# Graph attention with one level of Strassen products: v's seventh product ahead of t's third, and another order of the prologue

## The chip, the cores and the metric

The kernel runs on one core of one Trainium2 chip. The metric is the device time of one execution in microseconds; several executions are made and their median is given.

## The reference

For each of 64 graphs of 128 nodes with 512 features (x is 64 x 128 x 512, adj 64 x 128 x 128):

```
h      = relu(layernorm(x))
output = h @ weight
alpha  = (h @ wq) @ (h @ wk)^T
alpha  = softmax(max(alpha, 0) * (adj != 0), over the first node axis)
result = x + alpha @ output
```

The three weights are 512 x 512 and everything is float32.

## The kernel before, in words

**Tiles and groups.** Four graphs make a group (GB = 4), so there are 16 groups, g = 0 to 15. The product of wq and wk^T is made once and called m; then t = h m and the scores are t h^T, while v = h weight. Each float32 operand of a matmul is split in two float16 parts, high and low (hn_hi and hn_lo for h, w_hi and w_lo, m_hi and m_lo, tT_hi and tT_lo, v_hi and v_lo, p_hi and p_lo for the probabilities), and each product is three matmuls: high by high, high by low, low by high. The high part is a rounding (a copy to float16), the low part is the difference.

**Strassen products.** For groups 2 to 14 t and v are made in quadrants by seven products each (P1 to P7) in place of eight. They need four sums of quadrants of h (S1 to S4, in s32), and of m and of weight (T1 to T4, in mt32 and wt32), each split in high and low as well. P7 is S3 by T3, P3 is S4 by a quadrant of the weights, P4 is a quadrant of h by T4. Between the products the banks are added: c22_t and c22_v are P1 + P6 + P7 + P5 of t and of v, made by DVE (lines 752 and 761) out of bank TB or VB, to which P4 is then added to form the last quadrant; so P4 of v waits for c22_v. Groups 0, 1 and 15 use whole products (whole_product_v, whole_product_t).

**The period.** One period of TensorE (g = 2 to 14) is: P1 and P5 of t, P1 and P5 of v, P2 and P6 of t, P2 and P6 of v, the four output products of the group before (outs), P7, P3 of t, P7 of v, P4 of t, P3 and P4 of v, and the scores. Around it in the same period, by orders written out by hand for each engine:

- ACT (from line 597) copies P1 and P5, makes the exponentials of the group before (line 579), rounds the quadrants of t and v (lines 540 to 570: t11, v11, t22, t12, v22, t21, v12, v21), makes h of group g+2 by the normalising activation (normalise_h, line 487), rounds it (hi_of_h, line 497) and rounds the sums of h (hi_of_sum, line 502).
- DVE (from line 799) masks the scores (alpha, line 776), takes the maxima (779), scales them (shift_max, 781), inverts the row sums (787, 792), takes the statistics of x for g+2 (721, 724), makes the sums of the products (747, 757, 752, 761), the low parts of t (735) and v (740), and adds the output to x (residual, 796).
- POOL normalises the probabilities (probs, p_hi, p_lo, lines 407 to 412), makes the scale and the shift of the layer norm (363 to 370), the low parts of h (375), the sums S1, S3, S2, S4 (383 to 394) and their low parts (401).
- SP issues all loads, the DMA transposes of the parts of h and of the mask, and the stores.

**The prologue.** Lines 636 to 694 of ACT, from 846 on in DVE, from 425 in POOL and from 1155 in TensorE: wk and wq are transposed, m is made in banks 0 to 3, power-of-two scales are found (w_scale is scale step 5, m_scale step 6), and w, m, T1 to T4 of both are split. DVE makes w_hi (892) and w_lo (894); ACT m_hi (650) and the float32 copy m32 (651), DVE m_lo (906); POOL the sums of w (440 to 446), DVE the sums of m (914 to 919); ACT rounds both, DVE takes the lows (wt_lo 927, mt_lo 936). TensorE makes v and t of group 0 (lines 1112 to 1114 and 1121 to 1123), scores of 0, t of 1, outs of 0, v of 1 (each waits for a residual of group 0, line 796, whose bank it takes), scores of 1, and then the first period. x_sb[:, 3] holds m32 until the sums of m are made; then x of group 3 is loaded into it.

Of the kernel before, what the change touches and what calls it, by code (L numbers as in the profile page):

```python
# [5 lines left out]
def graph_attention_kernel(nc, x, adj, weight, wq, wk, out):  # L6
# [18 lines left out]
    K = D // N  # L25
# [52 lines left out]
    with ctx:  # L78
# [88 lines left out]
        V_BANK = [[bank[VB][:], bank[VE][:], bank[FREE][:], s_flat if g == 0 else bank[TA][:]] for g in range(2)]  # L167
# [179 lines left out]
        def _(pool):  # L347
# [91 lines left out]
            pool.wait_ge(w_loaded, 16)  # L439
            nc.gpsimd.tensor_tensor(wt32[:, T1], w_sb[:, 0:HK, HD:], w_sb[:, 0:HK, :HD], ALU.subtract).then_inc(wt_summed, 1)  # L440
            nc.gpsimd.tensor_tensor(wt32[:, T3], w_sb[:, HK:, HD:], w_sb[:, 0:HK, HD:], ALU.subtract).then_inc(wt_summed, 1)
            pool.wait_ge(wt_summed, 1)
            nc.gpsimd.tensor_tensor(wt32[:, T2], w_sb[:, HK:, HD:], wt32[:, T1], ALU.subtract).then_inc(wt_summed, 1)
            layernorm_scales(1)
            pool.wait_ge(wt_summed, 3)
            nc.gpsimd.tensor_tensor(wt32[:, T4], w_sb[:, HK:, :HD], wt32[:, T2], ALU.subtract).then_inc(wt_summed, 1)
            for b in range(GB):
                lo_of_h(1, 1, b)
            layernorm_scales(2)
            sums_of_h(2, 0)  # L450
            normalise(0)
            lows_of_sums(2, 0)
# [20 lines left out]
        def _(act):  # L473
# [108 lines left out]
            def hi_of_whole_v(g, b):  # L582

                act.wait_ge(whole_v, whole(g, b + 1))
                if later(g):
                    act.wait_ge(out_filled, GB * g)
                nc.scalar.activation(v_hi[:, b], V_BANK[g > 0][b], ACT.Copy, scale=T_SCALE).then_inc(v_hi_made, 1)

# [8 lines left out]
            def period(i, j, nxt2=True, nxt2_sums=True):  # L597

                g = i * UNROLL + j
                s2 = (j + 2) % UNROLL  # L600

                def hi_of_h2(b):
                    hi_of_h(g + 2, j % 2, b, turn(i, j), sum_turn(i, j))

                copy_p1_t(g)
                exponentials(g - 1)
                copy_p5_t(g)
                copy_p1_v(g)
# [36 lines left out]


            act.wait_ge(scale_step, 6)
# [10 lines left out]
            for b in range(1, GB):  # L658
                hi_of_whole_v(0, b)
            act.wait_ge(wt_summed, 4)  # L660
            for f in range(4):
                nc.scalar.activation(wt_hi[:, f], wt32[:, f], ACT.Copy, scale=w_scale[:]).then_inc(wt_hi_made, 1)
            hi_of_whole_t(0, 0)
            hi_of_whole_t(0, 1)
            normalise_h(2, 2, 0)
            normalise_h(2, 2, 1)
            hi_of_whole_t(0, 2)
            normalise_h(2, 2, 2)
            normalise_h(2, 2, 3)
            hi_of_whole_t(0, 3)  # L670
            for b in range(GB):
                act.wait_ge(hT0_landed[b], 2 * 16)
                hi_of_h(2, 0, b)
            exponentials(0)
            act.wait_ge(mt_summed, 4)
            hi_of_whole_t(1, 0)
# [8 lines left out]
            hi_of_whole_t(1, 3)  # L685
            for b in range(GB):
# [4 lines left out]
            hi_of_whole_v(1, 0)  # L691
            hi_of_whole_v(1, 1)
            hi_of_sum(3, 1, 0, S1)
            hi_of_sum(3, 1, 1, S3)
            hi_of_whole_v(1, 2)
            hi_of_sum(3, 1, 2, S2)
            hi_of_sum(3, 1, 3, S4)
            hi_of_whole_v(1, 3)
# [15 lines left out]
        def _(vec):  # L714
# [120 lines left out]
            def lo_of_whole_v(g, b):  # L835
                vec.wait_ge(v_hi_made, GB * g + b + 1)
                nc.vector.scalar_tensor_tensor(v_lo[:, b], V_BANK[g > 0][b], T_SCALE, v_hi[:, b], ALU.mult,
                                               ALU.subtract).then_inc(v_split, 1)
# [20 lines left out]
            for b in range(GB):  # L859
# [28 lines left out]
            nc.vector.scalar_tensor_tensor(m_scale[:], ipow2[:, 1:2], m_factor, ipow2[:, 2:3], ALU.mult,  # L888
                                           ALU.mult).then_inc(scale_step, 1)
# [6 lines left out]
            stats_all(1, 1, 2)  # L896
            stats_all(1, 1, 3)
# [3 lines left out]
                                           pow2[:, 2:3], ALU.mult, ALU.mult).then_inc(scale_step, 1)  # L901
            for k in range(K):

                vec.wait_ge(m_hi_made, k + 1)
                vec.wait_ge(m_copied, k + 1)
# [4 lines left out]
            for b in range(GB):  # L910
                stats_all(2, 2, b)
            lo_of_whole_v(0, 0)

            nc.vector.tensor_tensor(mt32[:, T1], m32[:, 0:HK, HD:], m32[:, 0:HK, :HD], ALU.subtract).then_inc(mt_summed, 1)
            nc.vector.tensor_tensor(mt32[:, T3], m32[:, HK:, HD:], m32[:, 0:HK, HD:], ALU.subtract).then_inc(mt_summed, 1)
            vec.wait_ge(mt_summed, 1)
            nc.vector.tensor_tensor(mt32[:, T2], m32[:, HK:, HD:], mt32[:, T1], ALU.subtract).then_inc(mt_summed, 1)
            vec.wait_ge(mt_summed, 3)
            nc.vector.tensor_tensor(mt32[:, T4], m32[:, HK:, :HD], mt32[:, T2], ALU.subtract).then_inc(mt_summed, 1)
            for b in range(1, GB):  # L920
                lo_of_whole_v(0, b)
            for c in range(K):
                lo_of_whole_t(0, c)
            softmax_shift(0, 0, 1)
            for f in range(4):
# [39 lines left out]
        def _(pe):  # L965
# [73 lines left out]
            def period(i, j):  # L1039
# [66 lines left out]
            def whole_product_v(g, b):  # L1106

                s, dst = g % 2, V_BANK[g > 0][b]
# [36 lines left out]
            for b in range(GB):  # L1145
# [69 lines left out]
```

## Time and profile before

| what | us |
|---|---|
| median of 3 runs | 441.36 |
| lowest and highest run | 439.41, 442.39 |
| profiled execution | 444.44 |
| its span in the trace | 442.6 |
| TensorE busy | 412.1 |

The span is what the trace shows from the first to the last instruction; the time of the execution holds 1.8 us more around it. The granted TensorE clock was 0.987 of full speed over the span. Times in the rows are microseconds from the start of the span, "mean ns" and "ns" are said where they stand; PE is TensorE's matmul, DVE VectorE, ACT ScalarE, POOL GpSimd, SPq the queue of SyncE. An L with a number is a line of the kernel.

### The profile page before, as it was taken

The numbers are of one execution on the slowest core, as the hardware profiler recorded it, in microseconds if no ns is written. First come the engines' busy times: TensorE is split into PE (matmuls) and PEld (weight loads), VectorE is DVE, ScalarE is ACT, GpSimd is POOL, SyncE is SP. The second block draws the span as 40 slices with busy tenths as digits, with TensorE's granted clock in tenths as the row PEclk, the third lists the DMA queues.
The fourth block names the chain that finished last, engine by engine and source line by source line (L and its number), as shares of the span: only waits on it lengthen the run. The fifth ranks groups of instructions, "written<-read, shape, count | busy, mean of one in ns | idle before, by whom it ended". The sixth has DMA issues, their size and how long they took to land.

```text
span 442.6 us, 9188 instructions
## 1 busy us (share of the span) xinstructions
PE 412.1 (93%) x3499; PEld 313.9 (71%) x3499; DVE 300.6 (68%) x512; ACT 252.3 (57%) x513; POOL 296.7 (67%) x311
## 2 busy tenths in 40 slices
PE   6979894999999989999998999898998999899996
PEld 4424531497978777887978787787978787888452
DVE  4899499177677758677676768586676778637354
ACT  4548671648564665758565655748565655543331
POOL 0458497967779596987778795977778795320211
PEclk9989997899999999999999999999999999999999
DMA  8943755678869959798867879797787879263022
GB/s 300 327 86 59 205 109 121 185 145 196 195 171 176 240 143 182 226 160 249 156 193 163 200 173 208 168 182 236 138 194 167 192 180 219 44 96 108 0 97 96
DMA packets 157368, 73.97 MB, mean 167 GB/s; under 512 B 131216, under 2 KB 139408, under 8 KB 157328
## 3 DMA queue, kind: packets, MB, share of 16 engines
q1 hardware_dynamic: 156752, 72.37, 70.6%
q10 hardware_dynamic: 576, 1.05, 0.7%
q8 instruction: 27, 0.44, 0.4%
q14 instruction: 13, 0.11, 0.1%
HBM read 24.12 MB, written 16.78 MB: 92 GB/s over the span
## 4 chain that ended last, share of the span: by engine, by line
POOL 40%; PE 25%; issue 18%; DVE 9%; ACT 7%; DMA 1%; POOLq 0%; ACTq 0%; DVEq 0%
POOL hn_lo L375 12%; POOL hn_lo L401 8%; POOL s L390 4%; POOL inv_std L366 3%; POOL p_hi L410 3%; PE bank L1112 2%; PE bank L1114 2%; PE bank L1113 2%; POOL s L394 2%; POOL s L383 2%; ACT hn_hi L497 2%; ACT exps L579 2%; PE bank L1121 2%; PE bank L1122 2%; PE bank L1123 2%
## 5 line engine op out<-in xcount | busy, mean ns | idle before, releaser
L375 POOL TENSOR_TENSOR hn_lo<-h,hn_hi 128x512 f16<-128x512 f32 x64 | 79.3, 1249 | 39.4 <-ACT hn_hi L497 38.2
L487 ACT ACTIVATE h<-x_sb,shift,rstd 128x512 f32<-128x512 f32 x64 | 50.0, 806 | 59.7 <-POOL shift L370 59.7
L1002 PE MATMUL bank<-wt_hi,hT_hi 128*128 128x256 f16 x208 | 56.8, 273 | 10.2 <-DVE spare L761 10.2
L407 POOL TENSOR_TENSOR probs<-exps,row_inv 128x512 f32<-128x512 f32 x16 | 16.8, 1048 | 72.5 <-DVE row_inv L792 72.5
L740 DVE SCALAR_TENSOR_TENSOR v_lo<-bank,v_hi 128x512 f16<-128x512 f32 x39 | 26.7, 686 | 52.7 <-ACT v_hi L570 27.7
L401 POOL TENSOR_TENSOR hn_lo<-s,hn_hi 128x512 f16<-128x512 f32 x52 | 59.9, 1186 | 0.0
L1004 PE MATMUL bank<-wt_lo,hT_hi 128*128 128x256 f16 x208 | 56.7, 273 | 0.0
L1005 PE MATMUL bank<-wt_hi,hT_lo 128*128 128x256 f16 x208 | 56.7, 273 | 0.0
L987 PE MATMUL bank<-hT_hi,mt_hi 128*128 128x256 f16 x208 | 56.7, 273 | 0.0
L989 PE MATMUL bank<-hT_lo,mt_hi 128*128 128x256 f16 x208 | 56.7, 273 | 0.0
L990 PE MATMUL bank<-hT_hi,mt_lo 128*128 128x256 f16 x208 | 56.7, 273 | 0.0
L579 ACT ACTIVATE exps<-alpha,shift_max,s_unscale 128x128 f32<-128x128 f32 x64 | 30.9, 485 | 30.3 <-DVE shift_max L781 30.3
L1016 PE MATMUL s_bank<-tT_hi,hT_hi 128*128 128x128 f16 x256 | 43.7, 219 | 1.5 <-DVE tT_lo L842 1.5
L1017 PE MATMUL s_bank<-tT_lo,hT_hi 128*128 128x128 f16 x256 | 43.7, 219 | 0.0
L1018 PE MATMUL s_bank<-tT_hi,hT_lo 128*128 128x128 f16 x256 | 43.7, 219 | 0.0
L502 ACT ACTIVATE hn_hi<-s 128x512 f16<-128x512 f32 x52 | 32.0, 629 | 19.2 <-POOL s L390 10.8
L1004 PE MATMUL bank<-w_lo,hT_hi 128*128 128x256 f16 x156 | 42.5, 273 | 0.0
L1005 PE MATMUL bank<-w_hi,hT_lo 128*128 128x256 f16 x156 | 42.5, 273 | 0.0
L989 PE MATMUL bank<-hT_lo,m_hi 128*128 128x256 f16 x156 | 42.5, 273 | 0.0
L987 PE MATMUL bank<-hT_hi,m_hi 128*128 128x256 f16 x156 | 42.5, 273 | 0.0
L990 PE MATMUL bank<-hT_hi,m_lo 128*128 128x256 f16 x156 | 42.5, 273 | 0.0
L1002 PE MATMUL bank<-w_hi,hT_hi 128*128 128x256 f16 x156 | 42.5, 273 | 0.0
(148 smaller groups left out, 1165.4 us busy)
## 6 DMA issues: line engine op xcount, KB each, us to landing
x_sb<-in_x SPq DMA_DIRECT2D x16, 1024.0 KB, 5.6
out_h<-x_sb SPq DMA_DIRECT2D x64, 256.0 KB, 2.1
adj_sb<-in_adj SPq DMA_DIRECT2D x16, 256.0 KB, 5.3
w_sb<-in_L_gnn_weight SPq DMA_DIRECT2D x1, 1024.0 KB, 11.1
hn_lo<-in_L_gnn_wk ACTq DMA_DIRECT2D x2, 256.0 KB, 3.8
hn_lo<-in_L_gnn_wk SPq DMA_DIRECT2D x2, 256.0 KB, 3.6
hn_hi<-in_L_gnn_wq SPq DMA_DIRECT2D x2, 256.0 KB, 5.9
hn_hi<-in_L_gnn_wq ACTq DMA_DIRECT2D x2, 256.0 KB, 6.5
```

Of the source, the lines that this page charges most:

```text
L375: nc.gpsimd.tensor_tensor(hn_lo[:, s, b], h[:, b], hn_hi[:, s, b], ALU.subtract).then_inc(h_split, 1)
L401: nc.gpsimd.tensor_tensor(low, s32[:, f], high, ALU.subtract).then_inc(s_split, 1)
L487: nc.scalar.activation(h[:, b], x_sb[:, s, b], ACT.Relu, bias=shift[:, b:b + 1], scale=rstd[:, b:b + 1]).then_inc(h_made, 1)
L987: nc.tensor.matmul(o, bh[:, k, cols], ah[:, :, k], start=first and c == 0 and k == 0, stop=False, skip_group_check=True)
L989: nc.tensor.matmul(o, bh[:, k, cols], al[:, :, k], start=False, stop=False, skip_group_check=True)
L990: last = nc.tensor.matmul(o, bl[:, k, cols], ah[:, :, k], start=False, stop=k == HK - 1, skip_group_check=True)
L1002: nc.tensor.matmul(o, ah[:, r, k], bh[:, k], start=first and r == 0 and k == 0, stop=False, skip_group_check=True)
L1004: nc.tensor.matmul(o, ah[:, r, k], bl[:, k], start=False, stop=False, skip_group_check=True)
L1005: last = nc.tensor.matmul(o, al[:, r, k], bh[:, k], start=False, stop=k == HK - 1, skip_group_check=True)
L1016: nc.tensor.matmul(o, hT_hi[:, s, b, k], tT_hi[:, k, b], start=k == 0, stop=False)
L1017: nc.tensor.matmul(o, hT_hi[:, s, b, k], tT_lo[:, k, b], start=False, stop=False)
L1018: last = nc.tensor.matmul(o, hT_lo[:, s, b, k], tT_hi[:, k, b], start=False, stop=k == K - 1)
```

## The change

The arithmetic stays the same. Orders on all the engines change, and two kinds of operations move to another engine.

In the period, TensorE:

```diff
                 pe.wait_ge(t_summed, done(g, 1))
                 product_t(s, N_P7, bank[TB][:], False)
-                product_t(s, N_P3, bank[TE][:], False)
 
                 pe.wait_ge(v_summed, done(g, 1))
                 product_v(s, N_P7, bank[VB][:], False)
+                product_t(s, N_P3, bank[TE][:], False)
```

ACT and DVE in the period:

```diff
                     normalise_h(g + 2, s2, 1)
                     hi_of_h2(0)
                     normalise_h(g + 2, s2, 2)
+                hi_of_v11(g)
+                if nxt2:
                     hi_of_h2(1)
                     normalise_h(g + 2, s2, 3)
                     hi_of_h2(2)
-                    hi_of_h2(3)
-                hi_of_v11(g)
                 hi_of_t22(g)
                 hi_of_t12(g)
+                if nxt2:
+                    hi_of_h2(3)
                 if nxt2_sums:
                     hi_of_sum(g + 2, j % 2, 0, S1)
                     hi_of_sum(g + 2, j % 2, 1, S3)
+                hi_of_t21(g)
                 hi_of_v22(g)
-                hi_of_t21(g)
                 hi_of_v12(g)
                 if nxt2_sums:
                     hi_of_sum(g + 2, j % 2, 2, S2)
+                hi_of_v21(g)
+                if nxt2_sums:
                     hi_of_sum(g + 2, j % 2, 3, S4)
-                hi_of_v21(g)
```

```diff
                 sum_c22_t(g)
                 lo_of_v(g, 0, bank[VA][:], 0, 0)
+                sum_c22_v(g)
                 lo_of_t(g, 1, c22_t, 1, 1)
                 lo_of_t(g, 2, bank[TE][:], 0, 1)
-                sum_c22_v(g)
+                lo_of_t(g, 3, bank[TB][:], 1, 0)
                 lo_of_v(g, 1, c22_v, 1, 1)
-                lo_of_t(g, 3, bank[TB][:], 1, 0)
                 lo_of_v(g, 2, bank[VE][:], 0, 1)
                 lo_of_v(g, 3, bank[VB][:], 1, 0)
```

In the prologue ACT makes w_hi, and the copies of m come behind the roundings, the last one behind group 1's h:

```diff
+            act.wait_ge(scale_step, 5)
+            for k in range(K):
+                nc.scalar.activation(w_hi[:, k], w_sb[:, k], ACT.Copy, scale=w_scale[:]).then_inc(w_hi_made, 1)
 
             act.wait_ge(scale_step, 6)
             for k in range(K):
                 act.wait_ge(m_filled, k + 1)
                 nc.scalar.activation(m_hi[:, k], M_BANK[k], ACT.Copy, scale=m_scale[:]).then_inc(m_hi_made, 1)
-                nc.scalar.activation(m32[:, k], M_BANK[k], ACT.Copy, scale=m_scale[:]).then_inc(m_copied, 1)
-            hi_of_whole_v(0, 0)
+            for k in range(K - 1):
+                copy_m(k)
             for b in range(GB):
                 normalise_h(1, 1, b)
...
+            copy_m(K - 1)
```

POOL waits with the sums of w until the weights are split, and takes the sums of m over from DVE; normalising the probabilities of group 0 moves ahead of the second half of group 2's lows and sums:

```diff
-            pool.wait_ge(w_loaded, 16)
+            pool.wait_ge(w_split, K)
             nc.gpsimd.tensor_tensor(wt32[:, T1], w_sb[:, 0:HK, HD:], w_sb[:, 0:HK, :HD], ALU.subtract).then_inc(wt_summed, 1)
             nc.gpsimd.tensor_tensor(wt32[:, T3], w_sb[:, HK:, HD:], w_sb[:, 0:HK, HD:], ALU.subtract).then_inc(wt_summed, 1)
+            layernorm_scales(1)
             pool.wait_ge(wt_summed, 1)
             nc.gpsimd.tensor_tensor(wt32[:, T2], w_sb[:, HK:, HD:], wt32[:, T1], ALU.subtract).then_inc(wt_summed, 1)
-            layernorm_scales(1)
...
+            pool.wait_ge(m_copied, K)
+            nc.gpsimd.tensor_tensor(mt32[:, T1], m32[:, 0:HK, HD:], m32[:, 0:HK, :HD], ALU.subtract).then_inc(mt_summed, 1)
+            nc.gpsimd.tensor_tensor(mt32[:, T3], m32[:, HK:, HD:], m32[:, 0:HK, HD:], ALU.subtract).then_inc(mt_summed, 1)
+            pool.wait_ge(mt_summed, 1)
+            nc.gpsimd.tensor_tensor(mt32[:, T2], m32[:, HK:, HD:], mt32[:, T1], ALU.subtract).then_inc(mt_summed, 1)
             layernorm_scales(2)
-            sums_of_h(2, 0)
+            pool.wait_ge(mt_summed, 3)
+            nc.gpsimd.tensor_tensor(mt32[:, T4], m32[:, HK:, :HD], mt32[:, T2], ALU.subtract).then_inc(mt_summed, 1)
+            lo_of_h(2, 0, 0)
+            lo_of_h(2, 0, 1)
+            sum_s1(2)
+            sum_s3(2)
             normalise(0)
+            lo_of_h(2, 0, 2)
+            lo_of_h(2, 0, 3)
+            sum_s2(2)
+            sum_s4(2)
```

On DVE the scale of m comes behind w_lo; of group 1 the residuals of group 0 come ahead of mt_lo:

```diff
             vec.wait_ge(scale_step, 5)
             for k in range(K):
-                nc.vector.tensor_scalar(w_hi[:, k], w_sb[:, k], w_scale[:], None, ALU.mult).then_inc(w_hi_made, 1)
                 vec.wait_ge(w_hi_made, k + 1)
                 nc.vector.scalar_tensor_tensor(w_lo[:, k], w_sb[:, k], w_scale[:], w_hi[:, k], ALU.mult,
                                                ALU.subtract).then_inc(w_split, 1)
...
             lo_of_whole_t(1, 1)
+            lo_of_whole_t(1, 2)
+            lo_of_whole_t(1, 3)
+            for b in range(GB):
+                residual(0, 0, b)
             for f in range(4):
                 vec.wait_ge(mt_hi_made, f + 1)
                 nc.vector.tensor_tensor(mt_lo[:, f], mt32[:, f], mt_hi[:, f], ALU.subtract).then_inc(mt_split, 1)
-            lo_of_whole_t(1, 2)
-            lo_of_whole_t(1, 3)
             make_mask(2, 0, 2)
-            for b in range(GB):
-                residual(0, 0, b)
```

And TensorE takes the fourth whole product of v of group 0 (now in bank TA, no longer in s_bank) behind t's whole products:

```diff
-            for b in range(GB):
+            for b in range(GB - 1):
                 pe.wait_ge(hT0_landed[b], 2 * 16)
                 whole_product_v(0, b)
 
+            pe.wait_ge(hT0_landed[GB - 1], 2 * 16)
             pe.wait_ge(m_split, K)
             for c in range(K):
+                pe.wait_ge(m_copied, c + 1)
                 whole_product_t(0, c)
 
-            pe.wait_ge(v_split, 4)
+            pe.wait_ge(t_split, 1)
+            whole_product_v(0, GB - 1)
             scores(0, 0, quadrants=False)
+
+            pe.wait_ge(v_split, GB)
```

The roundings and lows of groups 0 to 3 on ACT and DVE are put in an order that answers to this.

## Rows read from the trace of the kernel before

**Rows 1.** The page, busy time of each engine, share of the span, instructions.
```profile
PE 412.1 (93%) x3499; PEld 313.9 (71%) x3499; DVE 300.6 (68%) x512; ACT 252.3 (57%) x513; POOL 296.7 (67%) x311
```

**Rows 2.** Waits of TensorE: line, releaser, us in total, times, longest.
```profile
PE bank L1002 <- DVE spare L761: 10.2, 11, 1.5
```

**Rows 3.** Timeline of TensorE: start, duration, line, output and inputs, [idle before, releaser].
```profile
90.62 0.27 PE L987 MATMUL bank<-hT_hi,m_hi 128*128 128x256 f16 x1
...
101.10 0.38 PE L1023 MATMUL bank<-v_hi,p_hi 128*128 128x512 f16 x1
...
111.55 0.22 PE L1016 MATMUL s_bank<-tT_hi,hT_hi 128*128 128x128 f16 x1
...
114.23 0.27 PE L987 MATMUL bank<-hT_hi,m_hi 128*128 128x256 f16 x1
...
160.01 0.28 PE L1002 MATMUL bank<-wt_hi,hT_hi 128*128 128x256 f16 x1 [1.49 <-DVE spare L761]
...
184.12 0.28 PE L1002 MATMUL bank<-wt_hi,hT_hi 128*128 128x256 f16 x1 [0.32 <-DVE spare L761]
...
407.16 0.22 PE L1016 MATMUL s_bank<-tT_hi,hT_hi 128*128 128x128 f16 x1
```

**Rows 4.** Timeline of POOL, the first probs and one turn of the ring.
```profile
95.13 1.04 POOL L407 TENSOR_TENSOR probs<-exps,row_inv 128x512 f32<-128x512 f32 x1 [3.57 <-DVE row_inv L792]
...
169.92 1.04 POOL L407 TENSOR_TENSOR probs<-exps,row_inv 128x512 f32<-128x512 f32 x1 [1.54 <-DVE row_inv L792]
...
184.96 1.71 POOL L390 TENSOR_TENSOR s<-s,h 128x512 f32<-128x512 f32 x1
186.75 1.27 POOL L394 TENSOR_TENSOR s<-h,s 128x512 f32<-128x512 f32 x1
187.98 4.52 POOL L401 TENSOR_TENSOR hn_lo<-s,hn_hi 128x512 f16<-128x512 f32 x4
194.04 1.04 POOL L407 TENSOR_TENSOR probs<-exps,row_inv 128x512 f32<-128x512 f32 x1 [1.54 <-DVE row_inv L792]
```

**Rows 5.** Timeline of ACT in the same turn.
```profile
180.27 0.58 ACT L558 ACTIVATE v_hi<-bank 128x512 f16<-128x512 f32 x1
...
188.05 0.63 ACT L502 ACTIVATE hn_hi<-s 128x512 f16<-128x512 f32 x1 [0.72 <-POOL s L394]
```

**Rows 6.** Timeline of DVE, the same turn and one slower shift_max.
```profile
189.81 0.68 DVE L776 SCALAR_TENSOR_TENSOR alpha<-s_bank,maskT 128x512 f32<-128x512 f32 x1
...
191.25 0.23 DVE L781 TENSOR_SCALAR shift_max<-row_max,s_unscale 128x4 f32<-128x4 f32 x1
...
215.52 1.12 DVE L781 TENSOR_SCALAR shift_max<-row_max,s_unscale 128x4 f32<-128x4 f32 x1
```

**Rows 7.** The prologue: timelines of DVE, ACT, SP, TensorE; landing of hT_lo; a window with PEclk.
```profile
30.46 0.75 DVE L894 SCALAR_TENSOR_TENSOR w_lo<-w_sb,w_scale,w_hi 128x512 f16<-128x512 f32 x1
...
56.60 6.58 DVE L927 SCALAR_TENSOR_TENSOR wt_lo<-wt,w_scale,wt_hi 128x512 f16<-128x512 f32 x4
...
20.85 1.14 ACT L497 ACTIVATE hn_hi<-h 128x512 f16<-128x512 f32 x2
...
29.45 1.27 SPq L278 DMA_TRANSPOSE hT_lo<-hn_lo  x1
...
DMA to landing us min/median/max: 2.5/2.5/4.5
...
25.91 0.38 PE L1112 MATMUL bank<-w_hi,hT_hi 128*128 128x512 f16 x1 [1.02 <-DVE w_lo L894]
...
28.90 0.61 PE L1112 MATMUL bank<-w_hi,hT_hi 128*128 128x512 f16 x1 [2.18 <-DVE w_lo L894]
...
40.11 0.38 PE L1121 MATMUL bank<-hT_hi,m_hi 128*128 128x512 f16 x1
...
75.51 0.59 PE L1112 MATMUL bank<-w_hi,hT_hi 128*128 128x512 f16 x1 [5.86 <-DVE x_sb L796]
...
75.00:80.00 5.00, 4.49 (x12) 1.65 (x13) 2.34 (x4) 4.66 (x8) 2.69 (x5) 0.53 0.87 266
```

More of the change, by code:

```diff
@@ L166, in graph_attention_kernel @@
         M_BANK = [bank[k][:] for k in range(K)]
-        V_BANK = [[bank[VB][:], bank[VE][:], bank[FREE][:], s_flat if g == 0 else bank[TA][:]] for g in range(2)]
+        V_BANK = [bank[VB][:], bank[VE][:], bank[FREE][:], bank[TA][:]]
         def out_bank(g):
@@ L586, in hi_of_whole_v @@
                     act.wait_ge(out_filled, GB * g)
-                nc.scalar.activation(v_hi[:, b], V_BANK[g > 0][b], ACT.Copy, scale=T_SCALE).then_inc(v_hi_made, 1)
+                nc.scalar.activation(v_hi[:, b], V_BANK[b], ACT.Copy, scale=T_SCALE).then_inc(v_hi_made, 1)
             def hi_of_whole_t(g, c):
@@ L644, in _, with copy_m @@
             hi_of_h(0, 0, GB - 1)
+            def copy_m(k):
+                act.wait_ge(m_split, k + 1)
+                nc.scalar.activation(m32[:, k], M_BANK[k], ACT.Copy, scale=m_scale[:]).then_inc(m_copied, 1)
+            act.wait_ge(scale_step, 5)
+            for k in range(K):
+                nc.scalar.activation(w_hi[:, k], w_sb[:, k], ACT.Copy, scale=w_scale[:]).then_inc(w_hi_made, 1)
             act.wait_ge(scale_step, 6)
@@ L657, in _ @@
             hi_of_h(1, 1, GB - 1)
-            for b in range(1, GB):
-                hi_of_whole_v(0, b)
+            copy_m(K - 1)
+            hi_of_whole_t(0, 0)
+            hi_of_whole_v(0, 0)
+            hi_of_whole_v(0, 1)
+            hi_of_whole_t(0, 1)
+            hi_of_whole_v(0, 2)
             act.wait_ge(wt_summed, 4)
-            for f in range(4):
+            for f in range(2):
                 nc.scalar.activation(wt_hi[:, f], wt32[:, f], ACT.Copy, scale=w_scale[:]).then_inc(wt_hi_made, 1)
-            hi_of_whole_t(0, 0)
-            hi_of_whole_t(0, 1)
+            hi_of_whole_t(0, 2)
+            for f in range(2, 4):
+                nc.scalar.activation(wt_hi[:, f], wt32[:, f], ACT.Copy, scale=w_scale[:]).then_inc(wt_hi_made, 1)
+            hi_of_whole_t(0, 3)
             normalise_h(2, 2, 0)
             normalise_h(2, 2, 1)
-            hi_of_whole_t(0, 2)
+            hi_of_whole_v(0, 3)
+            act.wait_ge(hT0_landed[0], 2 * 16)
+            hi_of_h(2, 0, 0)
+            act.wait_ge(hT0_landed[1], 2 * 16)
+            hi_of_h(2, 0, 1)
             normalise_h(2, 2, 2)
             normalise_h(2, 2, 3)
-            hi_of_whole_t(0, 3)
-            for b in range(GB):
-                act.wait_ge(hT0_landed[b], 2 * 16)
-                hi_of_h(2, 0, b)
             exponentials(0)
+            act.wait_ge(hT0_landed[2], 2 * 16)
+            hi_of_h(2, 0, 2)
+            act.wait_ge(hT0_landed[3], 2 * 16)
+            hi_of_h(2, 0, 3)
+            hi_of_whole_t(1, 0)
             act.wait_ge(mt_summed, 4)
-            hi_of_whole_t(1, 0)
             for f in range(4):
@@ L685, in _ @@
             hi_of_whole_t(1, 3)
+            hi_of_whole_v(1, 0)
             for b in range(GB):
@@ L690, in _ @@
             hi_of_h(3, 1, GB - 1)
-            hi_of_whole_v(1, 0)
             hi_of_whole_v(1, 1)
+            hi_of_whole_v(1, 2)
             hi_of_sum(3, 1, 0, S1)
             hi_of_sum(3, 1, 1, S3)
-            hi_of_whole_v(1, 2)
+            hi_of_whole_v(1, 3)
             hi_of_sum(3, 1, 2, S2)
             hi_of_sum(3, 1, 3, S4)
-            hi_of_whole_v(1, 3)
             period(0, FIRST)
@@ L836, in lo_of_whole_v @@
                 vec.wait_ge(v_hi_made, GB * g + b + 1)
-                nc.vector.scalar_tensor_tensor(v_lo[:, b], V_BANK[g > 0][b], T_SCALE, v_hi[:, b], ALU.mult,
+                nc.vector.scalar_tensor_tensor(v_lo[:, b], V_BANK[b], T_SCALE, v_hi[:, b], ALU.mult,
                                                ALU.subtract).then_inc(v_split, 1)
@@ L887, in _ @@
             nc.vector.tensor_scalar(w_scale[:], ipow2[:, 0:1], w_factor, None, ALU.mult).then_inc(scale_step, 1)
-            nc.vector.scalar_tensor_tensor(m_scale[:], ipow2[:, 1:2], m_factor, ipow2[:, 2:3], ALU.mult,
-                                           ALU.mult).then_inc(scale_step, 1)
             vec.wait_ge(scale_step, 5)
             for k in range(K):
-                nc.vector.tensor_scalar(w_hi[:, k], w_sb[:, k], w_scale[:], None, ALU.mult).then_inc(w_hi_made, 1)
                 vec.wait_ge(w_hi_made, k + 1)
@@ L895, in _ @@
                                                ALU.subtract).then_inc(w_split, 1)
-            stats_all(1, 1, 2)
-            stats_all(1, 1, 3)
+            nc.vector.scalar_tensor_tensor(m_scale[:], ipow2[:, 1:2], m_factor, ipow2[:, 2:3], ALU.mult,
+                                           ALU.mult).then_inc(scale_step, 1)
             nc.vector.tensor_scalar(out_unscale[:], pow2[:, 0:1], 1.0 / (P_SCALE * H_SCALE * T_SCALE * w_factor), None,
@@ L901, in _ @@
                                            pow2[:, 2:3], ALU.mult, ALU.mult).then_inc(scale_step, 1)
+            stats_all(1, 1, 2)
+            stats_all(1, 1, 3)
+            vec.wait_ge(scale_step, 6)
             for k in range(K):
                 vec.wait_ge(m_hi_made, k + 1)
-                vec.wait_ge(m_copied, k + 1)
                 nc.vector.scalar_tensor_tensor(m_lo[:, k], M_BANK[k], m_scale[:], m_hi[:, k], ALU.mult,
@@ L911, in _ @@
                 stats_all(2, 2, b)
+            lo_of_whole_t(0, 0)
             lo_of_whole_v(0, 0)
[L914 to L923, printed above, removed]
+            lo_of_whole_v(0, 1)
+            lo_of_whole_t(0, 1)
+            lo_of_whole_v(0, 2)
+            for f in range(2):
+                vec.wait_ge(wt_hi_made, f + 1)
+                nc.vector.scalar_tensor_tensor(wt_lo[:, f], wt32[:, f], w_scale[:], wt_hi[:, f], ALU.mult,
+                                               ALU.subtract).then_inc(wt_split, 1)
+            lo_of_whole_t(0, 2)
+            lo_of_whole_t(0, 3)
+            lo_of_whole_v(0, 3)
+            vec.wait_ge(scale_step, SCALE_STEPS)
             softmax_shift(0, 0, 1)
-            for f in range(4):
+            for f in range(2, 4):
                 vec.wait_ge(wt_hi_made, f + 1)
@@ L1106, in whole_product_v @@
             def whole_product_v(g, b):
-                s, dst = g % 2, V_BANK[g > 0][b]
+                s, dst = g % 2, V_BANK[b]
                 for k in range(K):
@@ L1143, in _ @@
             product_m(3)
-            for b in range(GB):
+            for b in range(GB - 1):
                 pe.wait_ge(hT0_landed[b], 2 * 16)
                 whole_product_v(0, b)
+            pe.wait_ge(hT0_landed[GB - 1], 2 * 16)
             pe.wait_ge(m_split, K)
             for c in range(K):
+                pe.wait_ge(m_copied, c + 1)
                 whole_product_t(0, c)
-            pe.wait_ge(v_split, 4)
+            pe.wait_ge(t_split, 1)
+            whole_product_v(0, GB - 1)
             scores(0, 0, quadrants=False)
+            pe.wait_ge(v_split, GB)
             pe.wait_ge(hT_landed[1], 2 * 16)
```

## The prediction

> **What bounds the kernel now.** I read the page first, for which engine is full; then the waits of TensorE, for what stops it; then the timeline of TensorE, for the length of a period; then the timelines of the other engines over one period, for what releases it; last the prologue.
>
> TensorE is busy for 412.1 of 442.6 us, so what it loses in waits is nearly all there is to win without fewer matmuls [rows 1]. Its longest sum of waits is 10.2 us in 11 pieces: the first matmul of v's last product (P4) waits for c22_v, DVE's sum of line 761 [rows 2]; three more, of 5.86, 2.18 and 1.02 us, lie in the prologue [rows 7]. The period of g=2 has no wait: it starts at 90.62, its outs at 101.10, its scores at 111.55, and the next period at 114.23 [rows 3]. So eight products take 10.48 us, 1.31 each (12 matmuls, 0.109 each; one of 512 columns then 0.218), and a period that never waits takes 23.61. The thirteen periods with sums run from 90.62 to the scores of the last at 407.16; 13 times 23.61, less 2.68 for those scores, is 304.25, and the trace has 316.54: 12.3 us are lost in eleven of them (a wait is some 0.16 longer than its row, as the row counts from a modelled end). Two rows show both sizes, 1.49 and 0.32 [rows 3].
>
> What releases the wait is a ring of the other engines. From probs to probs POOL takes 24.12 us (169.92 to 194.04) [rows 4], which is 0.5 more than TensorE needs. Its links: POOL normalises the probabilities and makes the scale of the layer norm; ACT makes h and, only behind all eight operations on h, v_hi of the first quadrant at 180.27 [rows 5]; DVE then takes v_lo, two lows of t and c22_v. Meanwhile POOL goes through lows and sums of h to the end of S2 at 186.67 and of S4 at 188.02 [rows 4]; ACT rounds S4 at 188.05 and only then v21 [rows 5]; DVE's v_lo and then alpha follow at 189.81, though the scores, started 1.31 after the product of 184.12 and 2.68 long, had been there since about 188.2; shift_max, the exponentials and row_inv lead to the next probs [rows 4, 6]. In other periods shift_max takes 1.12 to 1.26 instead of 0.23 [rows 6], and the wait one product later in the ring is the long one. It began at 215.52 while POOL was within its four lows of sums, each 1.13; I read it as waiting for the one in progress. The Trainium skill, "SBUF — State Buffer", section "Who interferes with whom", says the same: a tensor_scalar in a two-port mode and an instruction with two SBUF inputs contend with GpSimd for one locked pair. By that rule moving mt's four sums to POOL frees DVE but buys new collisions with DVE's wt_lo; the trace agrees that such operations stretch.
>
> **Part 1, the product order in the period (thirteen times).** Nothing is added or taken on any engine; P7 of v ends one product, 1.31 us, earlier, at 15.7 instead of 17.0 us after the period's start; t's P3 ends 1.31 later. More matters the ACT order: v_hi of the first quadrant comes behind four operations on h instead of eight, some 2.3 us earlier (a rounding is 0.57 [rows 7]), and DVE takes c22_v straight after that v_lo, ahead of two lows of t (0.7 each by the nearest row, alpha [rows 6]). So c22_v comes at least 3.7 us sooner in the ring where the longest wait was 1.65. The wait goes. P4 then waits for nothing but the products before it, with some 2 us in hand.
>
> What is late next is the ring. ACT now rounds S4 behind v21, which waits for S2 only: S2's end instead of S4's, 1.35 us sooner. Against this, v_hi stands before the second rounding of h, so POOL's second low starts some 0.5 later (it now starts just when that rounding ends), and everything on POOL after it too. Alpha comes 0.85 sooner, 19.04 us behind probs where it was 19.89. shift_max, three links on, then falls in POOL's second low of a sum rather than near the end of the third; waiting for its end costs up to 0.3. The ring becomes 24.12 - 0.85 + 0.3, about 23.6, against TensorE's 23.61. That is a draw, and the slack decides: probs may come between 4.4 (scores bind) and 6.9 us (the second half of the scores needs the last low of t) after the start of a period before TensorE waits at all, so single slow turns are absorbed. Bounds: no wait left gives 12.3 us; a ring of 24.1 gives back 0.5 times 12, leaving 6. A ring that always misses a slot is a rival below. I take 2 us of remaining waits: **10.3 us won**.
>
> **Part 2, the prologue.** DVE now makes w_lo only, ACT w_hi, and POOL waits until the weights are split. The last w_lo of DVE ended at 31.21; TensorE, whose products of M end at 24.9, idled 1.02 and 2.18 us for the first two and then ran at 0.61 a matmul where 0.38 is usual [rows 7]. Now ACT's four w_hi (0.6 each, by its roundings of 0.57) run from 22.0, when group 0's last h is rounded, to 24.5 [rows 7]; w_lo's end at about 24.5, 25.2, 25.9 and 26.6. TensorE can go on almost without idling; the 3.2 us of waits and the slow matmuls after them go. Then the transposes of h are late next: the last is issued at 29.45 and takes 2.5 to land, 31.95 [rows 7]. Three whole products of v (2.6 each) run from 24.9 to 32.7, and as the fourth moves behind t's products, the first t product starts there if m is split. m_scale, now behind w_lo, comes at 26.7; ACT's m_hi end at 29.1; DVE's statistics and four m_lo end at 32.3, or 33.4 if m_scale waits for POOL. So t's products start at 32.7 to 33.4 where they did at 40.11 [rows 7]: 7 us sooner. m_copied of the last column comes behind group 1's h on ACT, at about 37.8, and is needed at 40.5: covered.
>
> From there TensorE has t (10.4), v's fourth (2.6), scores (2.7), t of group 1 (10.4) and outs (2.6): 28.7 us, so outs end at 61.4 if probabilities are there at 58.8. POOL's list (mt's sums 5.0, layer norm 2.0 to 2.7, T4, two lows, S1, S3) ends at 53; normalise gives p_lo at 57.3. Covered, by 1.5 us only; it starts this list at 38.9, when group 1's lows end (four lows of 1.13 behind the eight ACT operations on h, 5.0 us, which end at 37.2).
>
> Then v of group 1 needs the residuals of group 0. They stood behind four mt_lo of 5.42 us in all, and v began at 75.51 after 5.86 us idle [rows 7]. Now they come ahead of mt_lo but behind the last low of t, which on ACT is behind the rounding of S4: POOL's two lows, S2 and S4 end at 62.1, ACT and DVE need 1.8, a residual 0.7: v starts at 64.6, idle 3.2 us. Bounds: 63.0 if nothing collides, 67 if POOL's dozen operations each lose 0.3. The clock fell after the idle of before: 0.53 was granted from 75 to 80, the lower of the two levels, 1.2 and 2.4 GHz [rows 7]. I keep 2.1 us for it. Products 10.4, scores 2.7: the first period starts at 79.8 instead of 90.62. v_lo of group 1 (needed first) is at 79.3, mt_lo at 72.6; POOL's lows of group 3's sums end at 86.3, and probs with them (95.13 before [rows 4]): 6.4 us after the period's start, just inside the 6.9. **10.7 us won**, 7 to 13.5.
>
> **Part 3, the tail.** From the last period's scores at 407.16 to the end nothing is changed and TensorE was dense: 35.4 us stay.
>
> **Sum.** The profiled execution took 444.44 us with a span of 442.6. 444.44 - 10.3 - 10.7 = 423.4. The median of the runs, 441.36, is 3.1 us under the profiled one, which I keep: 420.4. Predicted: 420.5 us, 4.7% faster.
>
> **Rivals.**
> A, the ring stays the bound. For it: probs comes in only 0.5 us inside the limit at the first period, and 23.6 against 23.61 is closer than I can add. If each turn is 24.1 to 24.3 (the half microsecond on POOL's second low and a missed slot every second turn), 6 to 8 us are given back to TensorE's wait for the last t low or for p_lo: 426 to 428. Against it: TensorE's slack. 0.22.
>
> B, the prologue gives little. If m's split, POOL's list or group 0's residuals come 4 us later than I have them, the first period starts near 84 or 85: 425. For it: DVE's wt_lo collide with POOL there (6.58 us for four before). 0.12.
>
> C, the idle goes altogether, residuals by 62, clock never low: 415 to 417. 0.08.
>
> D, slower. POOL and DVE block each other more in the new order: the ring loses a whole slot of 1.13 twice each turn (shift_max, and one of DVE's two operations with two SBUF inputs, the lows of c22_t and c22_v, against S1 to S2). Place: alpha to probs and S1 to S2 on POOL. From a ring of 25.4 on, twelve turns eat the 8.8 us by which probs starts earlier (12 times 24.7 was the old average, 0.7 above is 8.4). At 25.9 it is 12 times 1.2 less 8.8: 447. For it, the stretched shift_max; against, that these collisions are in the 24.7 already. 0.03.
>
> E, the wait moves without gain because P3 of t now feeds its rounding late and holds up h's fourth rounding on ACT behind it: within 1%, 440. Against: that rounding comes at 18.1 us of the period where POOL wants it at about 20. 0.03.
>
> **How the numbers follow.** My case has 0.52, with its own range of 417 to 425. A, B and C fill up to 430 and down to 415; range 414 to 431. One per cent, 4.4 us, is about what the measurement can tell. Faster 0.94, same 0.03, slower 0.03.
>
> **What would show it.** Right: no wait of TensorE at P4 of v for c22_v; period starts 23.6 apart; first period at about 80; t's whole products from about 33; one wait near 62 to 65 ended by a residual. shift_max still long in some turns with TensorE unmoved. Wrong: period starts over 24.0 apart, with TensorE released by p_lo or t_lo (A); the first period after 83 (B).

## The result and the profile after

| what | us |
|---|---|
| changed kernel, median of 4 runs | 421.12 (420.80 to 421.59) |
| kernel before, median of 4 runs | 440.91 (439.41 to 442.39) |
| ratio | 0.9552, 95% interval 0.9517 to 0.9587 |
| profiled execution, and its span | 420.80, 419.0 (before 444.44, 442.6) |

The change makes the kernel 4.5% faster; 420.5 was forecast. Ratios here and below are those of the fast runs (less than 1.5% above the kernel's fastest), so they differ a little from the quotients of the medians shown. The page's busy times, against [rows 1]:

```profile
PE 406.6 (97%) x3499; PEld 314.8 (75%) x3499; DVE 282.9 (68%) x504; ACT 253.3 (60%) x517; POOL 298.2 (71%) x315
```

TensorE has the same 3499 matmuls and is now busy for 97% of the span. DVE has eight operations fewer (four w_hi, four sums of m) and ACT and POOL four more each. These are TensorE's waits, against [rows 2]:

```profile
PE bank L1121 <- DMA hn_lo<-in_L_gnn_wk: 4.2, 1, 4.2
PE bank L1149 <- DVE x_sb L833: 2.7, 1, 2.7
PE bank L1149 <- DMA hT_lo<-hn_lo: 0.9, 1, 0.9
PE bank L1024 <- DVE v_lo L874: 0.4, 1, 0.4
PE bank L1060 <- POOL p_lo L412: 0.2, 1, 0.2
```

The 10.2 us of waits for c22_v are gone. One wait for a residual is left (2.7, before 5.9). Before the first period there are 0.4 us of waiting for the last v_lo of group 1, and in all thirteen periods there is one wait, 0.2 us for p_lo. Lines have moved: on TensorE a line of before is 37 lines further down. TensorE's timeline, against [rows 3, 7]:

```profile
31.32 0.39 PE L1149 MATMUL bank<-w_hi,hT_hi 128*128 128x512 f16 x1 [0.86 <-DMA hT_lo<-hn_lo]
...
33.92 0.38 PE L1158 MATMUL bank<-hT_hi,m_hi 128*128 128x512 f16 x1
...
65.33 0.38 PE L1149 MATMUL bank<-w_hi,hT_hi 128*128 128x512 f16 x1 [2.67 <-DVE x_sb L833]
...
78.93 0.28 PE L1024 MATMUL bank<-hT_hi,m_hi 128*128 128x256 f16 x1 [0.40 <-DVE v_lo L874]
...
89.75 0.39 PE L1060 MATMUL bank<-v_hi,p_hi 128*128 128x512 f16 x1 [0.16 <-POOL p_lo L412]
...
102.89 0.27 PE L1024 MATMUL bank<-hT_hi,m_hi 128*128 128x256 f16 x1
...
126.50 0.27 PE L1024 MATMUL bank<-hT_hi,m_hi 128*128 128x256 f16 x1
...
383.53 0.22 PE L1053 MATMUL s_bank<-tT_hi,hT_hi 128*128 128x128 f16 x1
```

The first period begins at 78.93 instead of 90.62; the second lasts 23.61 (102.89 to 126.50), and the first 0.35 more, which holds the one wait; from the first start to the last scores there are 304.60 us instead of 316.54. So the span's 23.6 us are 11.7 of the prologue and 11.9 of the periods; the tail is 35.47 for 35.4.

One turn of the ring on POOL, ACT and DVE, against [rows 4 to 6]. POOL:

```profile
156.88 1.04 POOL L407 TENSOR_TENSOR probs<-exps,row_inv 128x512 f32<-128x512 f32 x1 [0.34 <-DVE row_inv L829]
...
166.12 1.16 POOL L375 TENSOR_TENSOR hn_lo<-h,hn_hi 128x512 f16<-128x512 f32 x1 [0.54 <-ACT hn_hi L512]
...
172.38 1.72 POOL L390 TENSOR_TENSOR s<-s,h 128x512 f32<-128x512 f32 x1
174.17 1.28 POOL L394 TENSOR_TENSOR s<-h,s 128x512 f32<-128x512 f32 x1
...
180.25 1.04 POOL L407 TENSOR_TENSOR probs<-exps,row_inv 128x512 f32<-128x512 f32 x1 [0.34 <-DVE row_inv L829]
```

ACT, the rounding of v21 now between those of S2 and S4; and DVE:

```profile
174.66 0.58 ACT L585 ACTIVATE v_hi<-bank 128x512 f16<-128x512 f32 x1
175.48 0.63 ACT L517 ACTIVATE hn_hi<-s 128x512 f16<-128x512 f32 x1 [0.24 <-POOL s L394]
```

```profile
153.95 0.38 DVE L818 TENSOR_SCALAR shift_max<-row_max,s_unscale 128x4 f32<-128x4 f32 x1
...
175.88 0.68 DVE L813 SCALAR_TENSOR_TENSOR alpha<-s_bank,maskT 128x512 f32<-128x512 f32 x1
```

This turn takes 23.37 us; the eleven from 86.24 to 344.16 take 23.45 on the mean (23.29 to 23.63), a little less than TensorE's 23.61. S2 ends 17.22 us after probs, alpha starts at 19.00, and POOL's second low waits 0.54 for the rounding that v_hi was put before: each as worked out. shift_max is 0.38 here, a short wait in place of 1.25 or none, and no shift_max of this profile takes over 0.54.

### The profile page after: what moved, and what is told of

Read it like the earlier page. It is cut to its first block, busy times and chain, and to the rows that moved or that the text cites. A ratio compares the mean times of both kernels' runs of the same rounds, so it can differ in the third digit from the quotient of the medians.

```text
span 419.0 us, 9187 instructions
## 1 busy us (share of the span) xinstructions
PE 406.6 (97%) x3499; PEld 314.8 (75%) x3499; DVE 282.9 (68%) x504; ACT 253.3 (60%) x517; POOL 298.2 (71%) x315
## 3 DMA queue, kind: packets, MB, share of 16 engines
q10 hardware_dynamic: 576, 1.05, 0.7%
## 4 chain that ended last, share of the span: by engine, by line
PE 81%; POOL 9%; DMA 3%; DVE 3%; ACT 1%; SPq 1%; issue 1%; DVEq 0%; POOLq 0%; ACTq 0%
PE bank L1041 9%; PE bank L1027 9%; PE bank L1026 9%; PE bank L1042 9%; PE bank L1024 9%; PE bank L1039 9%; PE s_bank L1055 3%; PE s_bank L1053 3%; PE s_bank L1054 3%; POOL hn_lo L375 2%; PE bank L1060 2%; PE bank L1062 2%; PE bank L1061 2%; DMA x_sb<-in_x 2%; POOL hn_lo L401 2%; PE bank L1160 2%
## 5 line engine op out<-in xcount | busy, mean ns | idle before, releaser
L375 POOL TENSOR_TENSOR hn_lo<-h,hn_hi 128x512 f16<-128x512 f32 x64 | 73.4, 1159 | 41.0 <-ACT hn_hi L512 40.7
L401 POOL TENSOR_TENSOR hn_lo<-s,hn_hi 128x512 f16<-128x512 f32 x52 | 58.6, 1159 | 0.0
L772 DVE SCALAR_TENSOR_TENSOR tT_lo<-bank,tT_hi 128x512 f16<-128x512 f32 x39 | 26.4, 676 | 23.4 <-ACT tT_hi L567 19.7
## 6 DMA issues: line engine op xcount, KB each, us to landing
w_sb<-in_L_gnn_weight SPq DMA_DIRECT2D x1, 1024.0 KB, 11.4
```

The lines of the kernel that those rows point to most:

```text
L375: nc.gpsimd.tensor_tensor(hn_lo[:, s, b], h[:, b], hn_hi[:, s, b], ALU.subtract).then_inc(h_split, 1)
L401: nc.gpsimd.tensor_tensor(low, s32[:, f], high, ALU.subtract).then_inc(s_split, 1)
```

## The experiments

All are compared with runs of the kernel before on the same chip, three sets on three chips; its median there was 444.06 for the first four experiments, 443.96 for the next four and 444.85 for the last three, so differences count, not only the absolute times.

**1. TensorE's product order alone, on the kernel before.**

```diff
                 product_t(s, N_P7, bank[TB][:], False)
-                product_t(s, N_P3, bank[TE][:], False)
                 pe.wait_ge(v_summed, done(g, 1))
                 product_v(s, N_P7, bank[VB][:], False)
+                product_t(s, N_P3, bank[TE][:], False)
```

> Only TensorE's product order of the period is changed on the kernel before (P7 of v ahead of P3 of t); ACT, DVE and the prologue are as before. Theory of the ring (TensorE's wait for c22_v is the end of a chain probs, h, v_hi, v_lo, lows of t, c22_v that no product of TensorE holds up): no change, 440 to 442 us, waits for c22_v still 9 to 11 us in sum. Rival, the product order itself: the sum of c22_v was late because its product was late, so each of the thirteen periods gains up to 1.31 us: 428 to 431 us, waits near zero.

Measured: 442.39 us (before 444.06; ratio 0.9956, 0.9916 to 0.9997). The exchange that names the change is worth some 2 us by itself (0.1 to 3.7 by the interval), where 12 were to be had if the product had been what was late. The wait stays:

```profile
PE bank L1002 <- DVE spare L761: 6.7, 9, 1.5
```

Its profile has four long shift_max, that of before seven. Fewer long turns make part of the smaller sum (experiment 8); whether the exchange gives a few tenths of a per cent besides is left open by an interval that ends 0.03% from no change.

**2. The changed kernel with the old product order** (the same edit the other way round).

> The changed kernel with TensorE's old product order (P3 of t ahead of P7 of v), all else changed. Ring theory: P7 of v then ends 17.0 us after the period's start, c22_v 0.8 later, and P4 of v begins at 19.6, so nothing waits: 421 to 422 us, period starts 23.61 apart. Rival, the product order: a good part of the 12 us of the periods comes back, 428 us or more.

Measured: 420.93 us (420.32 to 421.72), as the changed kernel. With the other orders in place the product order isn't needed either. Its periods start 23.6 us apart too.

**3. All three orders of the period, with the prologue of before.**

> All the changes of the period (TensorE, ACT and DVE), with the prologue of before. The first period then starts at about 90.6 us instead of 78.9, and later ones are 23.61 apart: 421.1 plus 11.7 is 432.8; I expect 431.5 to 434. Rival (the new prologue is what gives the periods their slack, so they still wait with the old one): 436 or more, with waits for p_lo, the lows of t or c22_v of 3 us and more.

Measured: 432.64 us (ratio 0.9724, 0.9668 to 0.978), no wait of TensorE in the periods and last scores at 395.65, as expected. The period's orders do not need the new prologue.

**4. The new prologue, with the period of before.**

> The new prologue, with the three orders of the period as before. Ring theory: from the first probs on the ring of the other engines sets the end, and probs comes 8.9 us sooner (86.24 against 95.13), so 440.9 less 8.9 is 432.0; 431 to 433.5. Rival, the gains add: TensorE's first period starts 11.7 us sooner and the waits of the periods stay as they were, so 429.2, 428.5 to 430.

Measured: 434.35 us, 9.7 us under the kernel before of that set (ratio 0.9759, 0.9704 to 0.9815). The absolute time missed my bracket by 0.9 because that kernel stood 3 us higher than I had counted on; the difference of the medians lies nearer the ring's 8.9 than 11.7, but the interval, 8 to 13 us, holds both. The trace decides. The first period starts 10.3 us sooner than before, the first probs 8.4 sooner, and waits for c22_v are there as before:

```profile
80.31 0.27 PE L1021 MATMUL bank<-hT_hi,m_hi 128*128 128x256 f16 x1
...
86.70 1.05 POOL L407 TENSOR_TENSOR probs<-exps,row_inv 128x512 f32<-128x512 f32 x1
```

```profile
PE bank L1036 <- DVE spare L795: 10.5, 12, 1.5
```

The last scores come at 397.41, 310.7 us behind the first probs; with six long shift_max in this profile that is as long as the kernel before would take with six (experiment 8). So what TensorE's earlier start has over the earlier probs is lost again in waits: the ring sets the end.

**5. One edit undone: S4 rounded ahead of v21.**

```diff
                     hi_of_sum(g + 2, j % 2, 2, S2)
-                hi_of_v21(g)
                 if nxt2_sums:
                     hi_of_sum(g + 2, j % 2, 3, S4)
+                hi_of_v21(g)
```

> The changed kernel with one edit undone: ACT rounds S4 ahead of v21 again, so that v_lo, alpha and the softmax wait for POOL's S4 and not for S2 only. Ring theory: the turn of the ring grows by 1.2 to 1.35 us, from 23.4 to 24.6 or 24.7, and is the bound again: some 1.0 us of wait a period on TensorE, 12 us less what slack is left: 430 to 433. Rival (the shorter wait of v_hi and c22_v alone was what counted, the softmax has slack): 421 to 422.5.

Measured: 441.91 us (439.44 to 443.06), some 20 us lost by one exchange of two roundings on ACT; the kernel before had 443.96 beside it (ratio 0.9954, 0.993 to 0.9979). Both expectations are wrong, the first by 9 us. DVE's shift_max:

```profile
157.82 0.68 DVE L813 SCALAR_TENSOR_TENSOR alpha<-s_bank,maskT 128x512 f32<-128x512 f32 x1
...
159.25 1.25 DVE L818 TENSOR_SCALAR shift_max<-row_max,s_unscale 128x4 f32<-128x4 f32 x1
...
183.40 0.68 DVE L813 SCALAR_TENSOR_TENSOR alpha<-s_bank,maskT 128x512 f32<-128x512 f32 x1
...
184.83 1.25 DVE L818 TENSOR_SCALAR shift_max<-row_max,s_unscale 128x4 f32<-128x4 f32 x1
```

POOL's four lows of sums in the second of these turns:

```profile
181.55 4.50 POOL L401 TENSOR_TENSOR hn_lo<-s,hn_hi 128x512 f16<-128x512 f32 x4
```

The last of them and shift_max both end at 186.1. Alpha is later by 1.35 us as expected, but shift_max now begins just inside another low of POOL in ten of the eleven turns from 107 to 363 us and lasts 1.1 to 1.26: turns of 25.6 on the mean, and 24.54 in the one without. The wait of TensorE is at a new place, the last v_lo of the group before, which v's first product needs:

```profile
PE bank L1039 <- DVE v_lo L777: 11.9, 11, 1.1
```

**6. The kernel before with shift_max made by ACT.** No other operation is moved; row_max is multiplied on ACT by a negative scale, which DVE makes once in the prologue (one 128x1 operation more).

```diff
+                act.wait_ge(scale_step, SCALE_STEPS)
+                act.wait_ge(max_found, g + 1)
+                nc.scalar.activation(shift_max[:], row_max[:], ACT.Copy, scale=neg_unscale[:]).then_inc(shift_made, 1)
...
-                vec.wait_ge(max_found, g + 1)
-                nc.vector.tensor_scalar(shift_max[:], row_max[:], s_unscale[:], -1.0, ALU.mult,
-                                        ALU.mult).then_inc(shift_made, 1)
```

> The kernel before with one operation moved: shift_max (128x4) is made by ACT from row_max instead of by DVE, with a negative scale made once. Theory of the lock (the 1.12 to 1.26 us turns are DVE waiting for the low of POOL that is in progress): no long turn is left, the ring turns in 24.1 to 24.3 us every time, seven slow turns of the profile go: 436 to 438.5, and the runs differ by under 1 us where they differed by 3. Rival (the long turns come from something else, as the write of row_max or the instruction stream): 440 to 443, and ACT's operation or its wait is long instead.

Measured: 439.59 us, 438.82 to 439.82, where the kernel before ran from 441.63 to 446.12 beside it (ratio 0.9904, 0.9869 to 0.994). ACT's operation takes 0.30 every time, there is no long turn, and the spread is 1.0 us (4 runs) for 4.5 (17 runs). TensorE's waits for c22_v are 4.7 us in ten pieces, so the ring is still the bound. The absolute time is 1.1 over my bracket; the turns average 24.28 where I had 24.1 to 24.3.

**7. A further change of the prologue**, on the changed kernel: POOL takes group 3's scales ahead of the lows of group 2's sums, ACT the rounding of group 1's last t ahead of those of S2 and S4.

```diff
-            lows_of_sums(2, 0)
             layernorm_scales(3)
+            lows_of_sums(2, 0)
+            pool.wait_ge(s_split, 4)
             sums_of_h(3, 1)
...
             hi_of_whole_t(1, 2)
+            hi_of_whole_t(1, 3)
             hi_of_sum(2, 0, 2, S2)
             hi_of_sum(2, 0, 3, S4)
-            hi_of_whole_t(1, 3)
```

The parts of v of group 1 also go between those of group 3's h.

> The changed kernel with a further change of the prologue: POOL makes group 3's layer norm scales ahead of the lows of group 2's sums, ACT rounds t's last part of group 1 ahead of S2 and S4, and v's parts of group 1 go between h's. By the chain of POOL, probs of the first period comes at 83.3 instead of 86.2, the wait of 2.67 us for a residual goes, and the first period starts near 75.6: 418 to 419. Rival (POOL's chain is not what starts the ring, or TensorE now waits in the first period for p_lo as much as it won): 420.5 to 421.5.

Measured: 422.68 us (420.55 to 423.23), no gain over the 421.12 and 421.74 of the changed kernel, which ran in other sets. The first period starts 2 us sooner, at 76.94, but TensorE then waits 2.3 us for p_lo. On DVE:

```profile
78.24 0.26 DVE L820 TENSOR_SCALAR shift_max<-row_max,s_unscale 128x4 f32<-128x4 f32 x1
85.24 1.29 DVE L760 BATCH_NORM_STATS2 raw_stats<-x_sb 128x6 f32<-128x512 f32 x2 [6.75 <-DMA x_sb<-in_x]
86.44 0.15 DVE L826 TENSOR_SCALAR row_sum_s<-row_sum 128x4 f32<-128x4 f32 x1
```

The lows, now later, delayed their transposes on SP's queue; behind those stands the load of group 4's x, DVE's statistics wait for it, and the row sums wait behind the statistics.

**8. The kernel before once more, for a second profile.**

> The kernel before, unchanged, for another profile of it. Lock theory: each run has its own number of long shift_max, seven in the first profile of 444.44 us; one of about 441 should show four or so, 1.1 us of time apiece. Rival: the number is the same and the difference lies elsewhere, in the prologue or in the DMA.

Measured: 445.21 us with eight long shift_max. With experiment 1's profile (whose ring is that of before) there are three points: 4 long turns and a span of 439.9, 7 and 442.6, 8 and 443.4, some 0.9 us for each. From the first probs to the last scores, which leaves the prologue out, there are four with experiment 4: 308.4, 310.7, 312.0 and 312.6 us with 4, 6, 7 and 8 long turns, some 1.05 for each. That answers the rival: the difference doesn't lie in the prologue. No profile here is of the kernel before at about 441 us; the one with four long turns, of a run of 441.67, is experiment 1's.

**9. Experiment 5 with shift_max on ACT.**

> The kernel of e5_v21_behind_s4 (S4 rounded ahead of v21) with shift_max made by ACT as in e6_shift_on_act. If e5's 21 us are two parts, 1.35 us a turn of later alpha and 1.1 us a turn of shift_max waiting for POOL's low in progress, the second part goes: turns of 24.6 to 24.9 instead of 25.6 to 25.8, some 12 us less than e5: 429 to 432. Rival (the order alone makes all of it): 440 to 442 as e5, turns still over 25.5.

Measured: 434.24 us (433.53 to 434.29), 7.7 us under experiment 5, 2 over my bracket. POOL's turn:

```profile
160.70 1.04 POOL L408 TENSOR_TENSOR probs<-exps,row_inv 128x512 f32<-128x512 f32 x1 [1.68 <-DVE row_inv L830]
185.37 1.04 POOL L408 TENSOR_TENSOR probs<-exps,row_inv 128x512 f32<-128x512 f32 x1 [1.67 <-DVE row_inv L830]
```

24.67 here, 24.75 on the mean of eleven, against 25.56 in experiment 5. Of that one's loss some 8 us are waiting for POOL and some 12 the later alpha (experiment 5 ran on another chip, so this split is good to a microsecond or so).

**10. Experiment 7 with the load ahead of the transposes** on SP's queue, for group 1's turn of it only.

```diff
-                    if g + 1 < LAST:
+                    if g + 1 < LAST and g > 1:
                         transpose_sums(g + 1)
                 store(g - 1)
...
                     load_x(g + 3)
+                if g == 1:
+                    transpose_sums(g + 1)
```

> The kernel of e7_earlier_scales, with SP storing group 0 and loading x of group 4 ahead of transposing group 2's sums. Theory: e7 lost because DVE's statistics waited 6.75 us for that load with softmax_sum queued behind; with the load issued some 5 us sooner probs of the first period is bound by POOL's lows alone, 85.5 against 86.2 in the changed kernel, while the first period starts at 76.9: TensorE waits some 1.4 us for p_lo, and 0.7 us are left: 420 to 420.7. Rival (the load is not what held e7): 422 to 423 again.

Measured: 419.29 us (419.06 to 419.41), faster than the changed kernel beside it (experiment 11), and by more than expected: probs of the first period came at 84.86 for 85.5, and the wait for p_lo is 0.86 in place of 2.3; that for v_lo stays at 0.66:

```profile
76.35 0.28 PE L1028 MATMUL bank<-hT_hi,m_hi 128*128 128x256 f16 x1 [0.66 <-DVE v_lo L878]
...
88.37 0.39 PE L1064 MATMUL bank<-v_hi,p_hi 128*128 128x512 f16 x1 [0.86 <-POOL p_lo L414]
```

**11. The changed kernel again**, on the chip of 9 and 10.

> The changed kernel, unchanged, beside the other two on one chip: 420.8 to 421.6.

Measured: 421.74 us (421.21 to 422.21). Experiment 10 is 2.45 us, 0.6%, faster. As it differs from experiment 7 (422.68) only in where the load and the transposes stand, it was the load that held that one back.

## Why the prediction was right, step by step

**The bound.** That TensorE's own order didn't hold c22_v up is shown by experiments 1 and 2: the exchange gives some 2 us without the other orders and nothing with them. That the ring of POOL, ACT and DVE did is shown by 4, 5, 6 and 9: what lengthens or shortens a turn moves the time, and what only starts TensorE sooner doesn't. The prediction still named P7's earlier end as a part of the gain; with the other orders in place that part is nothing.

**The ring after.** 19.04 us from probs to alpha were forecast and 19.00 measured. The 23.6 for a turn was some 0.15 too long, as shift_max waited 0.15 and not 0.3. TensorE's period is 23.61 as worked out, and of the 2 us of waits that I kept in the periods 0.35 came, all in the first: 11.9 won for 10.3. Rival A didn't come. Its sign was near, though: probs of the first period began at 86.24, as forecast (86.3), but 7.3 us after the period's start and not 6.4, so outside the 6.9 that were given as the limit, because TensorE started sooner than forecast. It cost only the one short wait.

**What I hadn't seen is how near it stood.** Experiment 5 shows that without rounding v21 before S4 nearly the whole gain is lost, the prologue's part too: alpha is 1.35 later, a turn is 24.7, and in ten of eleven turns shift_max adds about another 1.0. That is rival D's mechanism with one missed slot instead of two. Whether the earlier v_hi and c22_v would have been enough without it is answered (no, 441.91, and 434.24 without the waits for POOL); whether they are needed beside it was not tried. In the changed order shift_max begins near the end of a low and waits 0.15; in experiment 5 it begins just behind the start of one. The prediction had placed it rightly for its own order, but gave no price for an alpha 1.35 later.

**The prologue.** t's products began at 33.92, forecast 32.7 to 33.4, as the third pair of transposes released its product of v at 31.32 only, where I had it start at 30.1: an idle of 0.86. The split of m wasn't what bound them: m_lo ended at 31.1, where 32.3 or 33.4 were forecast. v of group 1 began at 65.33 for 64.6, after 2.67 us; POOL's S4 before it ended at 62.66 for 62.1. The first period began at 78.93 for 79.8: that delay of 0.7 and the wait of 0.4 for v_lo are outdone by the 2.1 us that I had kept for a lower clock, which never came. 11.7 won for 10.7. The same kernel's other profile (experiment 11) starts its first period at 79.71, has no wait in the periods and its last scores only 0.43 later, at 383.96; so up to 0.8 us of such a difference is the execution's, and probs, not TensorE's start, is near to binding there. What each of the prologue's edits gives by itself was not tried.

**The size.** Both gains were 1.0 to 1.6 us too small; for the profiled execution I had 423.4 and it was 420.8. The step that failed is the last one, that the median lies 3.1 us under the profiled execution "which I keep". By experiment 8 those 3.1 us are some three long turns of shift_max fewer than the seven of that profile; for the runs without a profile this is inferred, not shown. The changed kernel has no long turn and its runs lie within 0.8 us of each other, its profiled one 0.3 under their median. The two errors, 2.6 and 3.4 us, cancel, so that 420.5 came within 0.6 of the measured time is luck; the mechanism and the two gains carry the direction and the size to about 3 us.

**Each part alone.** By the medians, against 444.06, the periods' orders give 11.4 and the prologue 9.7; together, 444.85 to 421.74, it is 23.1. They nearly add.

## What to carry to other kernels

When one engine waits for another at the same place in every period, time one full turn of the engines behind it before touching the order of the one that waits: here the exchange of products did next to nothing, and moving one 128x512 rounding back to its old place on another engine lost nearly the whole gain. An order that has the ring just inside the bound can lose by a collision what it won: shift_max cost 0.15 us a turn in one order and about 1.0 in the other. Where a small DVE operation with a wide spread of durations stands in that turn, look at what POOL runs at that moment; moving it to ACT took 4.4 us away and, as far as four runs show, most of the spread. An engine's queue carries delays between groups that share no data: a transpose moved later held up a load, statistics and a softmax.

## What the runs showed of the hardware that was not expected

TensorE's clock. After 2.67 us of idle in the changed kernel the next matmuls took 0.38 us each and the window from 65 to 75 shows the 2.4 GHz level (1.00 granted):

```profile
65.00:75.00 10.00, 9.67 (x45) 4.42 (x46) 5.55 (x10) 5.55 (x10) 7.55 (x10) 1.00 0.81 201
```

Before, 5.86 us of idle were followed by the 1.2 GHz level (0.53 on the mean of 75 to 80), and so were two shorter idle times, 1.02 and 2.18, with three matmuls between them [rows 7]: 1.00 was granted from 25 to 28 us, 0.50 from 29 to 31. So the length of one idle time alone doesn't say what follows it.

The lock between POOL and DVE. A 128x4 operation of DVE, shift_max, takes 0.23 us, 0.38, or 1.1 to 1.26, by where it meets POOL's 1.13 us operations, and made by ACT 0.30 at most. The Trainium skill, "SBUF — State Buffer", section "Who interferes with whom", has the rule, that of GpSimd and a DVE instruction in a two-port mode the one which started first holds the pair of SBUF ports that both use for its whole instruction. The trace agrees: in experiment 5 shift_max starts inside POOL's low and both end at 186.1; whether shift_max runs in such a mode no run here shows. The runs add that the kernel before differs by 4 us from run to run without any change in its program, some 0.9 to 1.05 us for each long turn in the four profiles.

The same shows on DVE's larger operations. The four mt_lo took 5.42 us before, beside POOL's lows of sums (5.83 for the four), and take 2.54 now, beside 128x4 operations of POOL. Before and now:

```profile
67.75 5.42 DVE L936 TENSOR_TENSOR mt_lo<-spare,mt_hi 128x512 f16<-128x512 f32 x4
...
67.08 2.54 DVE L977 TENSOR_TENSOR mt_lo<-spare,mt_hi 128x512 f16<-128x512 f32 x4
```
